# A two-layer graph kernel: four near one-hot buffers, distances a pair ahead of the lanes, sums two superchunks behind, one-hots with the lane innermost, and index loads cut into 96 rows

## The chip, the cores and the metric

The kernel runs on one core of one Trainium2 chip. The metric is device time in microseconds (us). "Before" is the kernel as it stood, "after" the changed one. A core has five engines that run their own instruction streams and meet at semaphores: TensorE (PE, with its weight loads as PEld), VectorE (DVE), ScalarE (ACT), GpSimd (POOL) and SyncE (SP), which issues most of the DMAs.

## The reference, cut to what matters

```python
# x: (6250, 64); src, dst: (200000,), sorted by dst; edge_attr: (200000, 2, 64)
zmax = max(x, axis=-1)
e0, e1 = e[:, 0, :], e[:, 1, :]
q = 0.95 * zmax[src] * e1 + e0
sum_q, sum_ac = segment_sum(q, dst), segment_sum(e1, dst)
z_new = 0.2 * x + 0.8 * sum_q / (sum_ac + 1e-6)
x = layernorm(x + where(deg > 0, z_new, x))
# second layer: 4-head graph attention over the same edges with x @ Wq, x @ Wk, x @ Wv,
# softmax over the edges of one receiver, mean over heads, @ Wout
x = layernorm(x + gat(x))
```

The change touches only the first layer, above all the gather `zmax[src]` and the three segment sums (q, e1, and the degree), and the loads of `src` and `dst` at the start.

## The kernel before, in words

**Start.** SyncE loads `src` and `dst` as [98, 2048] words (196 superchunks of 1024 edges, two to a row): 97 full rows in one DMA, the last row, which holds 1344 words, in a second (L287 to L290). It then issues `x` (L292, L293) and the weights. VectorE turns `src` into two four-bit codes and their squared length (L558 to L568), which go to a DRAM scratch `codes_dram`, and `dst` into positions relative to a window of 24 nodes, plus tables of windows (L572 to L606). TensorE and ScalarE turn both around so that edges lie on partitions (L1194, L992). VectorE then waits for TensorE's turned `dst` (L615), makes the bf16 table of `zmax` in three parts (L627 to L633) and the loop starts.

**First layer.** One loop goes over the 196 superchunks t: 28 written out, then six turns of a body of 28. For one superchunk:

- SyncE loads its 512 KB of edge attributes into one of S1 = 7 slots (L327) and, every fourth, the code rows (L320).
- TensorE, `distances` (L1219): four matmuls, for two superchunks at a time, give the distance of every edge's code to each of 128 codes in PSUM (psD, all four of its banks hold one pair).
- ScalarE, `near_step` (L1014): two activations with Relu make of these the bf16 one-hot `near`, over 128 rows of the table of zmax. Two buffers.
- TensorE, `lanes` (L1225): 24 matmuls with `near` as weights and the table as moving operand give the 49 candidates of each edge in psZ.
- VectorE, `sums_step`: multiplies the candidates with the one-hot of the right lane (`picked`, L679, 392 elements), makes the one-hot of the receiver in its window (`hots`, L655), reduces `picked` to zmax per edge (`zm`, L685), adds sums that TensorE finished earlier into `acc` in two halves (L664), and between these makes the lane one-hot of the next superchunk (`hi_hots`, L659).
- GpSimd, `present_step`: weighs the receiver one-hot with zm (`hz_done`, L441) and counts degrees (L455 to L462).
- TensorE, `sums_of` (L1234): 64 matmuls with the edge attributes as weights and the two one-hots as moving operand.

**Order and waits.** Every engine's order is written out in the program. On TensorE step k is lanes(k), sums(k - 1), and on even k the distances of superchunks k + 2 and k + 3. The sums of k - 1 wait for GpSimd's product (`hz_done`) and for VectorE's adds (`add_done`), lanes(k) for ScalarE's near and for the pick of k - 2. ScalarE's near(k) waits for the pick of k - 2 (`sel_done`).

**After the loop** come the fold of the sums and the layer norm (to about 800 us) and the attention layer, which the change leaves alone.

## Time and profile before

| | |
|---|---|
| Time, median of 3 runs | 2893.26 us (2886.39 to 2896.32) |
| The profiled execution, own time | 2893.56 us |
| Its span, first to last instruction | 2891.3 us |
| Mean granted TensorE clock over the span | 0.709 |
| Busy over the span | PE 74%, PEld 54%, DVE 61%, ACT 45%, POOL 66% |
| Start, to the first lanes | 112.3 us |
| First layer's loop, 196 superchunks | 112 to 748 us |

The page gives shares over the whole span, in which the attention layer weighs most. The change lies in the first 750 us, so the two stages at the top of the list, the start and the loop, have to be read apart. A clock of 1.0 means the whole time at the higher of the two levels of TensorE's clock (2.4 GHz), 0.5 the whole time at the lower (1.2 GHz).

### The profile page before, as it was taken

The numbers are of one execution on the slowest core, as the hardware profiler recorded it, in microseconds if no ns is written. First come the engines' busy times: TensorE is split into PE (matmuls) and PEld (weight loads), VectorE is DVE, ScalarE is ACT, GpSimd is POOL, SyncE is SP. The second block draws the span as 40 slices with busy tenths as digits, with TensorE's granted clock in tenths as the row PEclk, the third lists the DMA queues.
The fourth block names the chain that finished last, engine by engine and source line by source line (L and its number), as shares of the span: only waits on it lengthen the run. The fifth ranks groups of instructions, "written<-read, shape, count | busy, mean of one in ns | idle before, by whom it ended". The sixth has DMA issues, their size and how long they took to land.

```text
span 2891.3 us, 78363 instructions
## 1 busy us (share of the span) xinstructions
PE 2144.7 (74%) x25183; PEld 1557.5 (54%) x25184; DVE 1768.1 (61%) x6022; ACT 1310.4 (45%) x3789; POOL 1896.0 (66%) x2644
## 2 busy tenths in 40 slices
PE   0476776666878787878877878878787877778875
PEld 0365665555746555545545555545565545555554
DVE  2676666676775655555556655655555555656568
ACT  0344333343364444444545544545444444545443
POOL 1355554455677777777777777777777777777750
PEclk9978777787675766676567666776656677776577
DMA  1455555455212122221222212222122221222111
GB/s 43 136 176 178 165 161 164 157 176 165 62 31 43 33 43 44 43 43 36 43 43 43 44 36 43 44 43 43 37 43 43 43 43 36 43 43 43 36 20 24
DMA packets 175709, 197.71 MB, mean 68 GB/s; under 512 B 95155, under 2 KB 97891, under 8 KB 173217
## 3 DMA queue, kind: packets, MB, share of 16 engines
q1 hardware_dynamic: 125030, 138.90, 16.8%
q0 software_dynamic: 50048, 51.35, 9.6%
q8 instruction: 280, 4.59, 0.7%
q14 instruction: 351, 2.88, 0.3%
HBM read 184.87 MB, written 5.25 MB: 66 GB/s over the span
## 4 chain that ended last, share of the span: by engine, by line
POOL 33%; PE 25%; issue 21%; DVE 9%; DMA 6%; SPq 3%; DVEq 1%; ACT 1%; ACTq 0%; POOLq 0%
POOL XS L518 32%; DMA XS<-x_dram,dst_bs 6%; PE psN L1234 3%; PE psS L1397 3%; PE psV L1356 3%; PE psM L1356 3%; PE psX L1225 2%; PE psM L1234 2%; PE psV L1225 2%; PE psT L1351 2%; DVE zm L685 1%; POOL XS L441 1%; DVE O L806 1%; PE psX L1346 1%; PE psN L1346 1%
## 5 line engine op out<-in xcount | busy, mean ns | idle before, releaser
L518 POOL DMA_INDIRECT XS<-x_dram,dst_bs x1564 | 1492.1, 954 | 487.9 <-issue 445.6
L803 DVE SCALAR_TENSOR_TENSOR l_st<-l_st,alpha,rsum 64x1 f32 x782 | 169.5, 217 | 552.7 <-PE psV L1356 279.7
L1397 PE MATMUL psS<-XT,Ubuf 96*128 96x512 f32 x522 | 417.1, 894 | 18.7 <-ACT Ubuf L1084 18.4
L875 DVE TENSOR_REDUCE rmax<-psS 128x1 f32<-128x512 f32 x391 | 270.2, 691 | 39.6 <-issue 16.2
L1356 PEld LDWEIGHTS psV<-XS,PT 128*128 128x128 f32 x1568 | 285.0, 271 | 1.4 <-ACT PT L1133 1.2
L1356 PE MATMUL psV<-XS,PT 128*128 128x64 f32 x1568 | 284.6, 346 | 0.7 <-ACT PT L1133 0.7
L1356 PEld LDWEIGHTS psM<-XS,dst_bs 128*128 128x128 f32 x1560 | 281.5, 270 | 1.6 <-ACT dst_bs L1133 1.6
L1356 PE MATMUL psM<-XS,dst_bs 128*128 128x64 f32 x1560 | 281.6, 345 | 0.7 <-ACT dst_bs L1133 0.7
L1133 ACT COPY PT<-psT 128x512 f32<-128x512 f32 x196 | 114.7, 585 | 349.6 <-PE psT L1351 349.0
L441 POOL TENSOR_TENSOR XS<-XS,zm 128x192 f32<-128x192 f32 x196 | 115.9, 592 | 239.1 <-DVE zm L685 237.7
L1133 ACT COPY dst_bs<-psT 128x512 f32<-128x512 f32 x195 | 114.1, 585 | 343.8 <-PE psT L1351 340.1
L1346 PEld LDWEIGHTS psX<-ident,XS 128*128 128x128 f32 x392 | 58.1, 184 | 390.1 <-issue 388.5
L1346 PEld LDWEIGHTS psN<-ident,XS 128*128 128x128 f32 x390 | 57.6, 183 | 380.8 <-issue 379.6
L1346 PE MATMUL psX<-ident,XS 128*128 128x128 f32 x392 | 108.5, 372 | 163.5 <-DMA XS<-x_dram,dst_bs 160.1
L1346 PE MATMUL psN<-ident,XS 128*128 128x128 f32 x390 | 107.1, 369 | 157.4 <-DMA XS<-x_dram,dst_bs 151.9
L1397 PE MATMUL psS<-dst_bs,Ubuf 96*128 96x512 f32 x260 | 210.0, 903 | 7.9 <-ACT Ubuf L1084 7.9
L1014 ACT ACTIVATE dst_bs<-psA,code_c 128x512 bf16<-128x512 f32 x98 | 67.3, 687 | 319.6 <-PE psT L1219 318.5
L1123 ACT ACTIVATE dst_bs<-psS,cur 128x512 f32<-128x512 f32 x195 | 134.0, 687 | 140.0 <-DVE cur L891 125.2
L1123 ACT ACTIVATE Pm<-psS,cur 128x512 f32<-128x512 f32 x196 | 134.7, 687 | 121.3 <-DVE cur L891 120.5
L797 DVE TENSOR_SCALAR XT<-big,win_ids 32x512 f32<-32x512 f32 x269 | 131.5, 489 | 73.6 <-issue 72.3
L1351 PE MATMUL psT<-ident,dst_bs 128*128 128x128 f32 x780 | 171.7, 362 | 5.1 <-ACT dst_bs L1123 4.8
L1351 PE MATMUL psT<-ident,Pm 128*128 128x128 f32 x784 | 173.1, 363 | 2.2 <-ACT Pm L1123 2.1
(276 smaller groups left out, 4408.6 us busy)
## 6 DMA issues: line engine op xcount, KB each, us to landing
big<-in_edge_attr_2x SPq DMA_DIRECT2D x195, 512.0 KB, 4.0
big<-dst_turned SPq DMA_DIRECT2D x49, 512.0 KB
XS<-x_dram,dst_bs POOLq DMA_INDIRECT x1564, 2.5
O<-codes_dram SPq DMA_DIRECT2D x200, 6.0 KB
x_dram<-x SPq DMA_DIRECT2D x12, 128.0 KB, 1.9
out<-big SPq DMA_DIRECT2D x12, 128.0 KB
codes_dram<-O SPq DMA_DIRECT2D x3, 392.0 KB
dst_turned<-big SPq DMA_DIRECT2D x1, 784.0 KB
```

Of the source, the lines that this page charges most:

```text
L441: return pool.tensor_tensor(buf[:, :, W:2 * W], buf[:, :, 0:W], z[:, :].unsqueeze(2).broadcast_to([P, SJ, W]), ALU.mult)
L518: pool.indirect_dma_start(xs(k, j), None, x1_dram, bass.IndirectOffsetOnAxis(ap=idx2[b % SB][:, k * CPP + j:k * CPP + j + 1], axis=0)).the ...
L797: dve.tensor_scalar(t[D:96, :], dst_b[J // S2 % SB][:, J % S2 * CH:(J % S2 + 1) * CH], ids, None, ALU.not_equal).then_inc(s, 1)
L803: dve.scalar_tensor_tensor(out=ls, in0=ls, scalar=al[half], in1=rs[half], op0=ALU.mult, op1=ALU.add)
L875: dve.tensor_reduce(rmax[:, q:q + 1], psSc[q][:, :], AX_X, ALU.max)
L1123: act.activation(Pms[a][:, :], psSc[a][:, :], ACT.Exp, bias=cur[:, a:a + 1], accum_out=rsum[:, a:a + 1]).then_inc(exp_done, 1)
L1133: act.copy(PTs[a][:, :], psT[:, :]).then_inc(pt_done, 1)
L1234: last = pe.matmul(ps[q * QT:(q + 1) * QT, h * 2 * W:h * 2 * W + n], e_sb[slot][:, h, c, q * QT:(q + 1) * QT], buf[:, j, 0:n], start=(c == ...
L1346: last = pe.transpose(psXc[b][:, j * P:(j + 1) * P], two, ident[:, :])
L1351: last = pe.transpose(ps[:, j * P:(j + 1) * P], probs[:, j * P:(j + 1) * P], ident[:, :])
L1356: last = pe.matmul(ps, pt[:, j * P:(j + 1) * P], xs(k, j), start=(j == 0), stop=(j == CPP - 1))
L1397: pe.matmul(psSc[1 - a][:, :], Ubuf[1 - a][:, :], XT[(J - 1) % 3][:, :], start=True, stop=True).then_inc(s_done, 1)
```

## The change

1. `near` has four buffers in place of two; ScalarE waits for the lanes of k - 4 (`z_done`), no longer for the pick of k - 2. `hz` has four buffers too.
2. TensorE's step k is: on even k the distances of k + 2 and k + 3, then lanes(k), then sums(k - 2). VectorE adds the sums of k - 3 in step k (before: k - 2).
3. `hi_hot` is laid out (edge group, lane) in place of (lane, edge group), so that the pick reads it in one run, and its making reads `hi_col` with the innermost step 0.
4. The [98, 2048] loads and stores are 96 rows, and the last two rows apart, each cut into 16 (or 8) pieces.

```diff
-        near = [dst_bs[:, k * CH:(k + 1) * CH].bitcast(BF16) for k in range(2)]
+        near = [t.bitcast(BF16) for t in (dst_bs[:, 0:CH], dst_bs[:, CH:2 * CH], XS[:, S2 * CPP * D - CH:S2 * CPP * D], dst_bs[:, 3 * CH:4 * CH])]
...
+            TM = TP_ // 16 * 16
+
+            def load_words(t, flat, done):
+                sp.dma_start(t[0:TM, :], flat[0:TM * RE].rearrange("(a b) -> a b", b=RE)).then_inc(done, 16)
+                for r in range(TM, TP_):
+                    n = RE if r < TP_ - 1 else LR
+                    sp.dma_start(t[r:r + 1, 0:n].rearrange("a (k e) -> a k e", k=16),
+                                 flat[r * RE:r * RE + n].rearrange("(a k e) -> a k e", a=1, k=16)).then_inc(done, 16)
+
             sp.wait_ge(s_init, 1)
-            sp.dma_start(src_raw[0:TP_ - 1, :], src[0:(TP_ - 1) * RE].rearrange("(a b) -> a b", b=RE)).then_inc(s_sall, 16)
...
+            load_words(src_raw, src, s_sall)
+            load_words(dst_raw, dst, s_dall)
...
-                    sp.wait_ge(seg_done, seg0 + (t - S1 + 3))
+                    sp.wait_ge(seg_done, seg0 + (t - S1 + 4))
...
-            for s, n in ((sel_done, 2), (hz_done, 1), (half_added, 2), (add_done, 3), (seg_done, 2), (deg_read, 2), (deg_done, 1), (s_pass, 1)):
+            for s, n in ((z_done, 4), (sel_done, 2), (hz_done, 2), (half_added, 3), (add_done, 4), (seg_done, 3), (deg_read, 2), (deg_done, 1), (s_pass, 1)):
...
             def hi_hots(t, q):
-                dve.tensor_tensor(hi_hot[q].rearrange("p (w j) -> p w j", j=SJ), lane_ids.rearrange("p (w j) -> p w j", j=SJ),
-                                  hi_col[:, bass.ds(t, 1), :].broadcast_to([P, LANES, SJ]), ALU.is_equal).then_inc(hi_done, 1)
+                dve.tensor_tensor(hi_hot[q].rearrange("p (j w) -> p j w", j=SJ), lane_ids.rearrange("p (j w) -> p j w", j=SJ),
+                                  hi_col[:, bass.ds(t, 1), :].rearrange("p s j -> p (s j)").unsqueeze(2).broadcast_to([P, SJ, LANES]), ALU.is_equal).then_inc(hi_done, 1)
...
-                dve.tensor_tensor(picked[k % 2].rearrange("p (j w) -> p j w", j=SJ), psZ[k % 2][:, 0:SJ * LANES].rearrange("p (j w) -> p j w", j=SJ),
-                                  hi_hot[k % 2].rearrange("p (w j) -> p j w", j=SJ), ALU.mult).then_inc(sel_done, 1)
+                dve.tensor_tensor(picked[k % 2], psZ[k % 2][:, 0:SJ * LANES], hi_hot[k % 2], ALU.mult).then_inc(sel_done, 1)
...
-                act.wait_ge(sel_done, vv)
+                act.wait_ge(z_done, vv)
...
-                pe.wait_ge(oh_done, vv)
-                pe.wait_ge(sel_done, vv)
-                lanes(k)
-                if not (isinstance(t, int) and t < 1):
-                    sums_step(k - 1, vv)
                 if k % 2 == 0:
                     u = (k + 2) // 2
                     nxt = pe.snap(vv + 1, min_val=1)
@@
                     pe.wait_ge(oh_done, nxt)
                     distances(u // 2 % RQ, u % 2)
+                pe.wait_ge(oh_done, vv)
+                pe.wait_ge(sel_done, vv)
+                lanes(k)
+                if not (isinstance(t, int) and t < 2):
+                    sums_step(k - 2, vv)
```

In the order of instructions, first SyncE at the start of the program, where the index words are loaded (97x2048 is partitions by words). Before:

```order
L287 DMA big<-in_src 97x2048
L288 DMA big<-in_src 1x1344
L289 DMA O<-in_dst 97x2048
L290 DMA O<-in_dst 1x1344
L292 DMA x<-in_x 128x48x64
```

After:

```order
L290 DMA big<-in_src 96x2048
L293 DMA big<-in_src 1x2048
L293 DMA big<-in_src 1x1344
L290 DMA O<-in_dst 96x2048
L293 DMA O<-in_dst 1x2048
L293 DMA O<-in_dst 1x1344
L300 DMA x<-in_x 128x48x64
```

Two more DMAs stand ahead of `x`, and the large ones have 96 partitions. Next TensorE at the start of the loop (psA, psS, psT and psS1, printed as psS, are the distances; psV and psX the lanes; psM the sums). Before:

```order
L1219 MATMUL psA<-O,code_w 128x512
L1219 MATMUL psS<-O,code_w 128x512 x2
L1219 MATMUL psT<-O,code_w 128x512
L1225 MATMUL psV<-table,dst_bs 128x49 x24
L1266 REGISTER_ALU
L1219 MATMUL psA<-O,code_w 128x512
L1219 MATMUL psS<-O,code_w 128x512 x2
L1219 MATMUL psT<-O,code_w 128x512
L1268 ISA
L1225 MATMUL psX<-table,dst_bs 128x49 x24
L1234 MATMUL psM<-XS,big 32x24 x2
```

After:

```order
L1230 MATMUL psT<-O,code_w 128x512
L1236 MATMUL psV<-table,dst_bs 128x49 x24
L1279 ISA
L1236 MATMUL psX<-table,dst_bs 128x49 x24
L1279 ISA
L1272 REGISTER_ALU
L1230 MATMUL psA<-O,code_w 128x512
L1230 MATMUL psS<-O,code_w 128x512 x2
L1230 MATMUL psT<-O,code_w 128x512
L1236 MATMUL psV<-table,XS 128x49 x24
L1245 MATMUL psM<-XS,big 32x24 x2
```

The first sums now stand behind the lanes of superchunk 2, not 1, and the distances ahead of the even lanes; the number of matmuls is the same. Last VectorE in the loop (Pm, PT: picked; XS: the receiver one-hot; PmX: the lane one-hot; big: acc). Before:

```order
L679 TENSOR_TENSOR Pm<-psV,PmX 128x392
L655 TENSOR_TENSOR XS<-win_rel,O 128x8x24
L685 TENSOR_REDUCE zm<-Pm 128x8
L664 ISA
L664 TENSOR_TENSOR big<-big,psM 128x2x24
L659 TENSOR_TENSOR PmX<-dst_bs,O 128x392
L664 ISA
L664 TENSOR_TENSOR big<-big,psM 128x2x24
```

After:

```order
L689 TENSOR_TENSOR PT<-psX,PmX 128x392
L665 TENSOR_TENSOR XS<-win_rel,O 128x8x24
L694 TENSOR_REDUCE zm<-PT 128x8
L674 ISA
L674 TENSOR_TENSOR big<-big,psM 128x2x24
L669 TENSOR_TENSOR PmX<-dst_bs,O 128x392
L674 ISA
L674 TENSOR_TENSOR big<-big,psM 128x2x24
```

The order within a step is the same; the sums in psM, of an even superchunk, are now added beside the pick of an odd one.

## Rows read from the trace of the kernel before

**Rows 1.** Busy time by stretch: PE, PEld, DVE, ACT, POOL (instructions), granted clock, DMA share, GB/s.

```profile
7.00:37.00 30.00, 0.00 (x0) 0.00 (x0) 0.55 (x2) 0.00 (x0) 8.56 (x2) 1.00 0.06 26
112.00:748.00 636.00, 448.55 (x17581) 371.86 (x17585) 432.06 (x1172) 250.56 (x392) 332.01 (x977) 0.79 0.53 169
```

**Rows 2.** Timeline, first two issues of SyncE (start us, us, what).

```profile
5.53 0.36 SPq L287 DMA_DIRECT2D big<-in_src  x1
5.95 8.29 SPq L288 DMA_DIRECT2D big<-in_src  x1
```

**Rows 3.** Timeline from the start to the first lanes.

```profile
4.88 10.64 POOL L428 MEMSET big<- 128x12640 f32 x1
...
37.70 1.23 DVE L558 TENSOR_SCALAR big<-big 98x2048 int32<-98x2048 int32 x1 [30.10 <-DMA big<-in_src]
...
70.38 1.23 DVE L572 CAST big<-O 98x2048 f32<-98x2048 int32 x1 [20.80 <-DMA O<-in_dst]
...
84.48 5.37 POOL L432 MEMSET O<- 128x6320 f32 x1 [68.92 <-DMA codes_dram<-O]
84.52 5.35 DVE L600 TENSOR_SCALAR lohi_i<-lohi_i 98x4 int32<-98x4 int32 x1
...
97.52 0.17 DVE L615 MEMSET big<- 128x128 f32 x1 [5.76 <-PE psM L1194]
...
112.33 1.18 PE L1225 MATMUL psV<-table,dst_bs 128*128 128x49 bf16 x24 [1.46 <-ACT dst_bs L1014]
```

**Rows 4.** Waits of TensorE in the loop (us in total, times, longest).

```profile
PE psN L1234 <- POOL XS L441: 25.0, 36, 1.8
PE psM L1234 <- POOL XS L441: 21.7, 30, 0.9
```

**Rows 5.** Timeline of TensorE, 298 to 308 us.

```profile
298.36 0.38 PE L1219 MATMUL psA<-O,code_w 3*128 3x512 bf16 x1
...
302.49 0.70 PE L1234 MATMUL psM<-XS,big 128*32 128x48 f32 x43 [1.76 <-issue]
303.13 0.82 PE L1225 MATMUL psV<-table,dst_bs 128*128 128x49 bf16 x24
303.87 1.35 PE L1234 MATMUL psN<-XS,big 128*32 128x24 f32 x59
306.19 0.38 PE L1234 MATMUL psN<-XS,big 128*32 128x24 f32 x5 [0.97 <-issue]
```

**Rows 6.** Timeline of TensorE, 464 to 476 us.

```profile
464.76 1.51 PE L1234 MATMUL psN<-XS,big 128*32 128x24 f32 x64
...
466.75 1.18 PE L1225 MATMUL psX<-table,dst_bs 128*128 128x49 bf16 x24
467.85 0.89 PE L1234 MATMUL psM<-XS,big 128*32 128x24 f32 x64
474.07 1.16 PE L1225 MATMUL psV<-table,dst_bs 128*128 128x49 bf16 x24 [5.33 <-issue]
```

**Rows 7.** Timeline of one superchunk's chain, all engines.

```profile
402.15 0.88 DVE L679 TENSOR_TENSOR Pm<-psV,PmX 128x392 f32<-128x392 f32 x1 [0.55 <-PE psV L1225]
...
403.33 0.56 DVE L685 TENSOR_REDUCE zm<-Pm 128x8 f32<-128x392 f32 x1
...
403.92 0.35 DVE L659 TENSOR_TENSOR PmX<-dst_bs,O 128x392 bf16<-128x392 bf16 x1
404.05 0.59 POOL L441 TENSOR_TENSOR XS<-XS,zm 128x192 f32<-128x192 f32 x1 [0.66 <-DVE zm L685]
...
404.19 0.20 DVE L664 TENSOR_TENSOR big<-big,psM 128x48 f32 x1
...
404.70 0.41 PEld L1234 LDWEIGHTS psM<-XS,big 128*32 128x32 f32 x34 [0.61 <-POOL XS L441]
```

**Rows 8.** DMA between 120 and 740 us: instruction queue, edge loads.

```profile
q8 instruction: 147, 2.41, 1.7%
...
big<-in_edge_attr_2x SPq DMA_DIRECT2D x187, 512.0 KB, 4.0
```

More of the change, by code:

```diff
@@ L51, in gnn_resnorm_kernel @@
     SB = 3
+    HB4 = 4
     U2 = 48
@@ L134, in gnn_resnorm_kernel @@
         hi_i = XS[0:TP_, 0:RE].bitcast(I32)
-        hz = [XS[:, k * SJ * 2 * W:(k + 1) * SJ * 2 * W].rearrange("p (j w) -> p j w", j=SJ) for k in range(3)]
-        hzX = hz[2]
+        hz = [XS[:, k * SJ * 2 * W:(k + 1) * SJ * 2 * W].rearrange("p (j w) -> p j w", j=SJ) for k in range(HB4)]
         dst_bs = sb("dst_bs", [P, 4 * CH], I32)
@@ L175, in gnn_resnorm_kernel @@
         relX = sb("relX", [P, SJ])
-        part = dst_bs[:, 3 * CH:3 * CH + 7 * W].bitcast(F32)
+        part2 = Pm[:, SJ * LANES:SJ * LANES + 4 * W]
+        part1 = PT[:, SJ * LANES:SJ * LANES + 2 * W]
         ones = sb("ones", [P, 1])
@@ L443, in present_step @@
             def present_step(t, k):
[L445 to L447 removed]
+                h2 = part2.rearrange("p (h j w) -> p h j w", h=2, j=2)
+                h1 = part1.rearrange("p (h w) -> p h w", h=2)
+                hot4 = hz[k % HB4].rearrange("p (h j) w -> p h j w", h=2)
                 vv = pool.snap(pcc, min_val=1)
@@ L690, in sums_step @@
                     dve.wait_ge(half_added, vv)
-                    add_sums(lb, psG[k % 2], 1).then_inc(add_done, 1)
+                    add_sums(lb, psG[(k + 1) % 2], 1).then_inc(add_done, 1)
                 dve.reg_add(tc, tc, 1)
@@ L1011, in near_step @@
                     act.reg_add(bc, bc, 1)
-                act.wait_ge(sel_done, vv)
+                act.wait_ge(z_done, vv)
                 for h in range(2):
-                    last = act.activation(near[k % 2][:, h * CH:(h + 1) * CH], psD[k % 2][h][:, :], ACT.Relu,
+                    last = act.activation(near[k % 4][:, h * CH:(h + 1) * CH], psD[k % 2][h][:, :], ACT.Relu,
                                           bias=code_c[:, 3:4], scale=-1.0)
@@ L1060, in keep_turned @@
                 act.copy(xt1[u % 2][0:rows_, 0:n], u_turn[u % 2][0:rows_, 0:n]).then_inc(s_xTc, 1)
-            act.wait_ge(s_dsts, 16)
+            act.wait_ge(s_dsts, 32)
             keep_turned(0)
@@ L1224, in lanes @@
                     for c in range(3):
-                        last = pe.matmul(psZ[k % 2][:, j * LANES:(j + 1) * LANES], near[k % 2][:, j * P:(j + 1) * P], table3[:, c, :],
+                        last = pe.matmul(psZ[k % 2][:, j * LANES:(j + 1) * LANES], near[k % 4][:, j * P:(j + 1) * P], table3[:, c, :],
                                          start=(c == 0), stop=(c == 2))
@@ L1284, in _ @@
                             step(i * UN + (HEAD + k), HEAD + k)
-                sums_step(NS - 1, pe.snap(pc, min_val=1))
+                left = pe.snap(pc, min_val=1)
+                sums_step(NS - 2, left)
+                sums_step(NS - 1, pe.snap(left + 1, min_val=1))
             pe.wait_ge(s_all1, 2)
```

62 lines of the change are left out of this document (30 added, 32 removed).

## The prediction, on record before the changed kernel ran

> **What bounds the kernel now.** I read the page for the stages, then busy time by stretch, then the timeline of the start, then TensorE's waits and its timeline in the loop. The change can act in two places: the 112.3 us ahead of the first lanes and the 636 us of the loop; behind 748 us the program is the same.
>
> At the start hardly anything computes. Between 7 and 37 us the DMA share is 0.06, one engine's worth of 16, and 26 GB/s flow [rows 1]: the load of `src` issued at 5.53 us [rows 2] is on one engine, and the first operation on it starts at 37.70 us, after 30.10 us of idle time. The same happens to `dst`: the cast L572 starts at 70.38 us after 20.80 us idle [rows 3]. Later VectorE waits 5.76 us at L615 for TensorE's turned `dst` [rows 3].
>
> In the loop TensorE is busy 448.6 of 636 us at a mean clock of 0.79 [rows 1], that is 58% of the time at the high level (0.5 + 0.5 x 0.58). The other 187 us are, by its waits, 46.7 us at the sums for GpSimd's product [rows 4], and nearly all the rest is "issue", for which the profile has no releaser. This issue time has two forms. One is in the middle of a group of equal matmuls: 1.76 us in front of 43 sums and 0.97 us in front of the last 5 of 64 [rows 5]. Between these two resumptions are 43 + 24 + 59 = 126 matmuls and 3.70 us. The instruction queue moved 147 blocks, 2.41 MB, in 620 us [rows 8], so one block of 16 KB per 4.2 us, about once for each such run of matmuls. I read these stalls as TensorE waiting for its next block of instructions. A superchunk has 24 + 64 + 2 = 90 matmuls, so a block holds 1.4 superchunks. The other form is the back edge of the body, 5.33 us [rows 6]; five of them are 27 us. What is left for blocks is 187.4 - 46.7 - 27, some 113 us, less a few for ScalarE.
>
> **The change part by part.** *Rows of 96.* No row shows 96 partitions. The bounds: as slow as 97 on one engine, no gain; or like the edge loads, 128 partitions and 512 KB landed 4.0 us after issue [rows 8], from which I estimate 6 us for 768 KB, so `src` is there at 12 us. I take the second. By the Trainium skill ("DMA: Bandwidth & Descriptors", the section "Why a DMA increments its semaphore by 16 and not by 1") a DMA runs on the largest number up to 16 that divides its slowest dimension: one for 97, which the share of 0.06 bears out, and 16 for 96; by it the load takes what I estimate from the edge loads, and no gain is excluded. GpSimd clears `acc` from 4.88 us for 10.64 us [rows 3]. L600, a tensor_scalar of 4 elements, took 5.35 us beside such a memset of 5.37 us [rows 3], so L558, a tensor_scalar too, will not end before the memset does, at 15.5 us, and its own 1.23 us: 16.7 us in place of 38.93. That is 22.2 us. The `src` chain ended 20.80 us ahead of 70.38, at 49.6 us; now at 27.4 us. `dst` has landed by then, the second large load behind the first, so L572 starts there: 43.0 us earlier. L600 stays behind a memset of GpSimd as before, since that waits for the same relative positions; no change. TensorE's second turn waited for `src` being turned, which hung on the weights that SyncE could issue only at 73 us. Now they are issued at about 11 us, and the idle 5.76 us at L615 go too. Together **48.7 us**, and the first lanes at 63.6 us. Bounds: 42 if SyncE's issues of loads run into each other as now (8.29 us for L288 [rows 2]), 53 if GpSimd's memset holds nothing up. The stores of 96 rows lie beside other work; nothing. More small DMAs: a handful of issues of 0.4 us [rows 2] on SyncE, which is then idle; nothing.
>
> *The chain of the sums.* At 402.15 us the pick starts, at 403.33 the reduce (0.56), at 404.05 GpSimd's product (0.59), and at 404.70 TensorE goes on, 0.61 us late: 2.55 us from pick to sums [rows 7]. With sums two behind, the product of k - 1 is no longer wanted, but the adds of step k - 1 still are, since `add_done` frees the PSUM bank. They end at 404.39 [rows 7], 2.24 us behind the pick. So the new release is the second add, 0.31 us sooner than the product, before the layout is counted.
>
> *Lane innermost.* The pick takes 0.88 us for 392 elements, the reduce of the same number 0.56 [rows 7]. Read in one run the pick should take between 0.56 and 0.88; I take 0.58. The making of the one-hot takes 0.35 us for the 392 now [rows 7]; it stays at 0.35 if the step of 0 costs nothing, and goes to 0.56, the pace of the reduce, if it does. I take 0.56, net 0.09 less per step. The skill ("Vector Engine (DVE) Microarchitecture Reference", section "5.1 Performance modes") speaks against this half of the change: two results a cycle want 16-bit operands with innermost step 1, and a two-source operation that read one element again and again ran at one a cycle. By it this edit alone adds 0.2 us times 196, 41 us of VectorE's time, and by the rows at most as much. On the path it is 0.31 + 0.30 - 0.21 = 0.40 us that the sums are released sooner, where the mean wait now is 46.7 us in 66 times, 0.71 us [rows 4]. A good half of the 46.7 us goes directly.
>
> *Four near buffers, distances first.* TensorE's waits for ScalarE are too few to have a row here; nothing directly. The distances now lead their lanes by two steps, and ScalarE, with four activations a pair, has the time. If it were late, TensorE would stop in front of the distances with lanes and sums queued behind; its work between two distances is 2 x (0.82 + 0.89) = 3.4 us at the high clock [rows 5, 6], and four activations are under 3 us.
>
> *What the loop then stands on.* TensorE's work per superchunk is 0.82 + 0.89 + 0.38/2 = 1.9 us at the high clock [rows 5, 6] and 1.18 + 1.51 + 0.3 = 3.0 us at the low one [rows 6]; the 0.3 is half of 0.38 scaled like the lanes. Instruction blocks allow one superchunk per 3.70/1.4 = 2.64 us at best. So the floor is 0.58 x 2.64 + 0.42 x 3.0 = 2.79 us, times 196 is 547, and 27 for the back edges: 574 against 636 us, **at most 62 us**. VectorE's step, 0.58 + 0.35 + 0.56 + 0.56 + 2 x 0.20 = 2.45 less the overlaps of about 0.1 each, is 2.1, below it. Of the 62 I take 43: half of the POOL waits, 24, and 19 because a wait inside a block also puts off the request for the next one. Bounds: 5, where every wait removed turns into a longer block stall, and 66.
>
> The tail gets one more group of sums, +1 us. The sum against the profiled execution's own 2893.6 us (0.3 above the median of the runs): 2893.6 - 48.7 - 43 + 1 = **2803 us**.
>
> **The rivals.** *The loop does not move*: blocks set the pace and shorter waits only lengthen stalls. For it: 113 us of stall are more than twice the POOL waits. Against: at the low clock TensorE has work for 1.4 x 3.0 = 4.2 us per block, more than 3.70, so waits there cost in full. It gives 2893.6 - 48.7 = 2845.
> *Blocks are no floor*: the stalls come from something that the decoupling removes, and the loop falls to VectorE's 2.1 at the high and TensorE's 3.0 at the low clock: 0.58 x 2.1 + 0.42 x 3.0 = 2.48, times 196 plus 27 is 513, 123 us less: 2723. Against: one block per run of 126 matmuls fits too well.
> *The start does not move*, as the loads stay narrow or `x` or the weights take their place: 2893.6 - 43 + 1 = 2852. For it: L288 alone blocked SyncE for 8.29 us [rows 2].
> *Slower*: the new rhythm keeps TensorE at the low clock. Each superchunk then costs 3.0 us of work in place of the mean 2.29 (448.6/196), and the idle 0.96 stays: 3.96 x 196 = 776, 140 us more, and 2893.6 + 140 - 48.7 = 2985. It decides from where work grows by the 48.7 us that the start gives: 0.25 us a superchunk, the high clock's share falling from 0.58 to about 0.36. Against: less waiting means a busier engine.
>
> **How the numbers follow.** Chances: the forecast 0.57, the loop unmoved 0.18, blocks no floor 0.09, the start unmoved 0.07, slower 0.04, and 0.05 for what I have not seen. The forecast's own range is 2780 to 2830. The range that leaves out two in ten goes from 2893.6 - 53 - 66 = 2775, a little lower for part of the second rival, to the unmoved start at 2852: 2770 to 2852. Within 0.3%, 8.7 us, a measurement of this kernel can't tell a difference from none; that both stages gain nothing has 0.03. Faster 0.93, same 0.03, slower 0.04.
>
> **What would show it.** Right: L572's successor starts near 27 us and the first lanes near 64; a pick of about 0.58 and a lane one-hot of 0.56 us; TensorE's waits for GpSimd gone, and fewer than 25 us for VectorE's adds in their place; stalls inside groups still there, at 3.7 us or more apart; a loop of about 593 us. Wrong: a DMA share of 0.06 at the start, ScalarE late in front of the distances, a clock well below 0.79 in the loop, or stalls gone.

## The result and the profile after

| | before | after |
|---|---|---|
| Time, median of 4 runs each | 2891.49 us (2886.39 to 2896.32) | 2856.12 us (2848.35 to 2856.7) |
| Ratio, 95% interval | | 0.9872 (0.9847 to 0.9896) |
| The profiled execution, own time | 2893.56 us | 2856.21 us |
| Span | 2891.3 us | 2853.6 us |
| First lanes, first row of TensorE's lanes in the timeline | 112.3 us | 65.2 us |
| Loop, from there to the first row of the fold | 640.0 us | 640.2 us |
| From the fold to the end | 2139.0 us | 2148.1 us |

The change gains 35 us of 2891, not the 90 that I forecast, and the median lies 4 us above my range. The start gives the gain (47.1 us); the loop gives nothing. The interval of the ratio leaves out 1, so the gain itself is clear of noise. The last row of the table is work that the change leaves alone; it came out between 2137.4 and 2153.6 us in the thirteen profiles taken on chips of this speed, and I take its 9 us as spread, which is argued and not shown.

The line of busy times of the page after:

```profile
PE 2168.6 (76%) x25183; PEld 1585.8 (56%) x25184; DVE 1756.7 (62%) x6022; ACT 1302.3 (46%) x3789; POOL 1940.1 (68%) x2644
```

The timeline of the start, all engines, which answers to [rows 2, 3]:

```profile
4.66 10.64 POOL L438 MEMSET big<- 128x12640 f32 x1
...
5.53 0.41 SPq L290 DMA_DIRECT2D big<-in_src  x1
6.00 0.59 SPq L293 DMA_DIRECT2D big<-in_src  x2
...
8.79 10.44 SPq L301 DMA_DIRECT2D x<-in_x  x1
11.20 5.22 DVE L568 TENSOR_SCALAR big<-big 98x2048 int32<-98x2048 int32 x1 [3.50 <-DMA big<-in_src]
...
19.27 1.00 SPq L303 DMA_DIRECT2D XT<-in_L_gnn_Wq  x1
...
27.21 1.23 DVE L582 CAST big<-O 98x2048 f32<-98x2048 int32 x1
...
39.58 5.37 POOL L442 MEMSET O<- 128x6320 f32 x1 [24.24 <-DVEq L594]
39.74 5.23 DVE L597 TENSOR_SCALAR wide<-wide 98x4 f32<-98x4 f32 x1
...
48.58 0.17 DVE L625 MEMSET big<- 128x128 f32 x1
...
65.23 1.18 PE L1236 MATMUL psV<-table,dst_bs 128*128 128x49 bf16 x24
```

`src` has landed at 11.20 us in place of 37.70. The first tensor_scalar lasts 5.22 us and ends at 16.4, 1.1 us behind the end of GpSimd's memset at 15.3, as the step said. The cast of `dst` starts at 27.21 us without a wait, and L625, which was L615 and stood behind 5.76 us of idle time [rows 3], has none.

Busy time by stretch, with the columns of [rows 1]: the start, and 636 us from the first lanes on.

```profile
7.00:37.00 30.00, 5.03 (x32) 4.33 (x32) 25.51 (x17) 6.46 (x8) 8.34 (x2) 1.00 0.63 154
65.00:701.00 636.00, 440.19 (x17632) 367.14 (x17629) 413.45 (x1174) 238.92 (x389) 372.46 (x980) 0.82 0.53 168
```

The DMA share of the start is 0.63 where it was 0.06. In the loop TensorE is busy 8 us less and VectorE 19 us less for the same work, and the stretch is as long. So idle time has taken the place of what went. TensorE's waits in the same stretch (us in total, times, longest):

```profile
PE psM L1245 <- issue: 77.7, 69, 2.8
PE psN L1245 <- issue: 52.0, 50, 3.7
PE psV L1236 <- issue: 23.6, 14, 3.6
PE psA L1230 <- issue: 20.0, 6, 4.0
PE psX L1236 <- issue: 15.4, 15, 2.5
PE psV L1236 <- ACT dst_bs L1025: 4.8, 3, 1.6
```

The rows for GpSimd, 25.0 and 21.7 us before [rows 4], are gone. The five rows of "issue" are 189 us. Under "issue" stand two things, stops in the middle of groups, and waits in front of sums whose releaser the profile doesn't name. Of the latter, all 46 in which the first weight load of the sums comes more than 0.12 us late end within 0.12 us of the end of one of VectorE's adds, as forecast; this is one of them:

```profile
284.18 0.20 DVE L674 TENSOR_TENSOR big<-big,psN 128x48 f32 x1
284.45 0.24 PEld L1245 LDWEIGHTS psN<-XS,big 128*32 128x32 f32 x13 [0.84 <-issue]
```

VectorE in the loop, by shape (busy us, mean ns, idle us before):

```profile
L669 DVE TENSOR_TENSOR PmX<-dst_bs,O 128x392 bf16<-128x392 bf16 x196 | 109.8, 560 | 0.0
...
L689 DVE TENSOR_TENSOR Pm<-psV,PmX 128x392 f32<-128x392 f32 x98 | 55.6, 567 | 122.7 <-PE psV L1236 122.4
```

Pick 0.567 us, lane one-hot 0.560, against the forecast 0.58 and 0.56.

For what follows I sorted every idle piece of TensorE in the loop of the trace, over 0.1 us, by the matmul or weight load on both sides: *in a group*, when they have the same line and destination; *in front of* a group otherwise; *long*, when over 3.2 us. What is left of the loop is work.

| us | loop | work | in groups | before sums | before lanes and distances | long |
|---|---|---|---|---|---|---|
| before | 640.0 | 451.3 | 108.2 | 46.9 | 8.2 | 25.3 |
| after | 640.2 | 443.1 | 141.9 | 18.8 | 14.1 | 22.4 |

The wait before sums shrank by 28 us, work by 8, the long pieces by 3. The stalls in groups grew by 34 and those before lanes and distances by 6, and the sum is zero. Before, the long pieces are the five back edges. After, four of the six are back edges, the other two (3.58 and 3.75 us) stand in the middle of groups, and the fifth back edge, 3.19 us, stands one column to the left.

### The profile page after: what moved, and what is told of

Same layout as the page of the kernel before. It is cut to its first block, busy times and chain, and to the rows that moved or that the text cites. A ratio compares the mean times of both kernels' runs of the same rounds, so it can differ in the third digit from the quotient of the medians.

```text
span 2853.6 us, 78268 instructions
## 1 busy us (share of the span) xinstructions
PE 2168.6 (76%) x25183; PEld 1585.8 (56%) x25184; DVE 1756.7 (62%) x6022; ACT 1302.3 (46%) x3789; POOL 1940.1 (68%) x2644
## 4 chain that ended last, share of the span: by engine, by line
POOL 35%; PE 29%; issue 21%; DVE 8%; DMA 5%; ACT 1%; DVEq 1%; ACTq 0%; SPq 0%; POOLq 0%
POOL XS L528 35%; DMA XS<-x_dram,dst_bs 5%; PE psM L1245 4%; PE psN L1245 4%; PE psS L1410 3%; PE psX L1236 3%; PE psV L1236 3%; PE psM L1369 3%; PE psV L1369 3%; PE psT L1364 1%; PE psA L1230 1%; DVE O L817 1%; PE psN L1359 1%; PE psX L1359 1%; DVE XS L758 1%
## 5 line engine op out<-in xcount | busy, mean ns | idle before, releaser
L1410 PE MATMUL psS<-XT,Ubuf 96*128 96x512 f32 x522 | 425.6, 911 | 20.0 <-ACT Ubuf L1095 19.3
L1369 PEld LDWEIGHTS psV<-XS,PT 128*128 128x128 f32 x1568 | 294.6, 279 | 1.4 <-ACT PT L1144 1.2
L1369 PE MATMUL psV<-XS,PT 128*128 128x64 f32 x1568 | 293.0, 353 | 0.7 <-ACT PT L1144 0.7
L1369 PEld LDWEIGHTS psM<-XS,dst_bs 128*128 128x128 f32 x1560 | 292.6, 279 | 1.6 <-ACT dst_bs L1144 1.6
L1369 PE MATMUL psM<-XS,dst_bs 128*128 128x64 f32 x1560 | 291.7, 354 | 0.7 <-ACT dst_bs L1144 0.7
L1144 ACT COPY PT<-psT 128x512 f32<-128x512 f32 x196 | 114.9, 586 | 357.8 <-PE psT L1364 357.2
L451 POOL TENSOR_TENSOR XS<-XS,zm 128x192 f32<-128x192 f32 x196 | 142.9, 729 | 194.4 <-DVE zm L694 185.4
L1134 ACT ACTIVATE dst_bs<-psS,cur 128x512 f32<-128x512 f32 x195 | 134.1, 687 | 137.7 <-DVE cur L902 120.8
L1245 PE MATMUL psM<-XS,big 128*32 128x24 f32 (+1 forms) x6272 | 120.0, 221 | 78.2 <-issue 77.7
```

Source lines behind the costliest of these rows:

```text
L451: return pool.tensor_tensor(buf[:, :, W:2 * W], buf[:, :, 0:W], z[:, :].unsqueeze(2).broadcast_to([P, SJ, W]), ALU.mult)
L1134: act.activation(Pms[a][:, :], psSc[a][:, :], ACT.Exp, bias=cur[:, a:a + 1], accum_out=rsum[:, a:a + 1]).then_inc(exp_done, 1)
L1144: act.copy(PTs[a][:, :], psT[:, :]).then_inc(pt_done, 1)
L1245: last = pe.matmul(ps[q * QT:(q + 1) * QT, h * 2 * W:h * 2 * W + n], e_sb[slot][:, h, c, q * QT:(q + 1) * QT], buf[:, j, 0:n], start=(c == ...
L1369: last = pe.matmul(ps, pt[:, j * P:(j + 1) * P], xs(k, j), start=(j == 0), stop=(j == CPP - 1))
L1410: pe.matmul(psSc[1 - a][:, :], Ubuf[1 - a][:, :], XT[(J - 1) % 3][:, :], start=True, stop=True).then_inc(s_done, 1)
```

## The experiments

All kernels below also carry the change's start (rows of 96) unless said. "Loop" and "in groups" are measured as above, on the profiled execution. Two profiles of the changed kernel gave loops of 640.2 and 635.9 us, two of the kernel with 64-column sums 512.7 and 508.8, so a difference under 5 us in one profile says little.

**1. The start alone, fewer instructions, no back edge.** Four kernels on one chip, whose runs of before have a median of 2892.28 us.

*b_rows96* is the kernel before with part 4 of the change alone.

> The kernel before with part 4 of the change alone (rows of 96). Both theories: the first lanes near 65 us in place of 112, the loop as before (640 us from the first lanes to the first fold), total about 2893 - 47 = 2846 us. If the loop moves too by over 5 us, the loads of the start reach into it and the accounting by stages is wrong.

Measured: 2846.74 us, ratio 0.9835 (0.981 to 0.9859); first lanes at 63.6 us, loop 631.2, in groups 103.7. The start alone gains 45.5 us where the whole change gained 35, though the intervals of the two ratios overlap. The loop missed what I expected: it is 9 us shorter than 640, and 5 was my limit, beyond which the accounting by stages would be wrong. From the fold to the end this profile has 2144.8 us, 6 more than before. So the total came out as worked out in part by luck, and why this loop is 9 us shorter is open; a difference of that size between loops of single profiles carries little.

*a_m64* is the changed kernel with the sums in half as many matmuls, each with 64 columns of edge attributes as weights in place of 32. The same sums are computed.

```diff
-                    for q in range(4):
-                        n = W if q < 2 else 2 * W
-                        last = pe.matmul(ps[q * QT:(q + 1) * QT, h * 2 * W:h * 2 * W + n], e_sb[slot][:, h, c, q * QT:(q + 1) * QT],
+                    for q in range(2):
+                        n = W if q < 1 else 2 * W
+                        last = pe.matmul(ps[q * D:(q + 1) * D, h * 2 * W:h * 2 * W + n], e_sb[slot][:, h, c, q * D:(q + 1) * D],
```

A superchunk has 24 + 64 + 2 = 90 matmuls, each with its weight load, so 180 instructions of this kind; now it has 58 and 116.

> The changed kernel with the sums in two column tiles of 64 in place of four of 32: the same numbers, 16 matmuls in the program where 32 stood, and per superchunk 116 records of matmuls and weight loads in place of 180; the columns that each part of the array streams stay the same. Theory 'instruction blocks pace the loop': a block now holds 2.1 superchunks, 3.7 us per block allow one per 1.7 us, so the work (1.9 us at the high clock, 3.0 at the low) and VectorE's 2.1 us are left; stalls inside groups fall from 149 us to under 40, the loop by 80 to 130 us, total 2730 to 2780. Rival 'two parts of the change cancel in the loop' (the new order costs what the shorter waits give): stalls in the middle of a group have nothing to do with instructions, the loop moves by under 15 us. Rival 'the edge loads pace it': no change at all.

Measured: 2720.97 us, ratio 0.9389 (0.9361 to 0.9417); loop 512.7, in groups 1.3. The loop falls by 127 us, within the 80 to 130 that I named; the total lies 9 us below my 2730 to 2780. TensorE in it, at a back edge and behind:

```profile
200.82 0.59 PE L1236 MATMUL psX<-table,dst_bs 128*128 128x49 bf16 x17
202.02 1.14 PE L1245 MATMUL psN<-XS,big 128*64 128x24 f32 x32 [0.61 <-POOL XS L451]
206.72 0.60 PE L1230 MATMUL psA<-O,code_w 3*128 3x512 bf16 x1 [3.56 <-issue]
...
207.27 1.18 PE L1236 MATMUL psV<-table,dst_bs 128*128 128x49 bf16 x24
208.38 1.95 PE L1245 MATMUL psM<-XS,big 128*64 128x24 f32 x32
```

A group of sums takes longer than with 64 narrow matmuls, at either level of the clock: 1.14 us against 0.89 and 1.95 against 1.51 [rows 6]. So the gain is not that the same sums became cheaper. The stops in groups fell by 141 us; the time in work fell by 23, at a higher clock, and 50 us came back as longer waits before sums (68.4 against 18.8). The instruction queue now moves 98 blocks between 73 and 560 us, one per 5.0 us, where it was one per 4.2 us. The wider window, 66 to 550 us, by engine:

```profile
66.00:550.00 484.00, 395.01 (x10824) 345.02 (x10821) 409.65 (x1118) 227.09 (x376) 350.66 (x933) 0.95 0.69 213
```

VectorE is busy 85% of it (409.65 of 484), TensorE 82% and at a granted clock of 0.95. Of the 171 waits before sums, 130 end within 0.12 us of the end of one of VectorE's adds and 41 behind GpSimd's product.

*b_m64* is b_rows96 with the same edit of the sums.

> The kernel before with part 4 and the sums in column tiles of 64, near one-hots and order as before. Theory 'instruction blocks': with the stalls gone the waits for GpSimd (47 us before) show in full, so the loop is shorter than before but 30 to 60 us longer than that of the changed kernel with the same sums. Rival 'parts cancel': both have the same loop within 10 us, whether or not it is shorter than 640.

Measured: 2748.11 us, ratio 0.9487 (0.9461 to 0.9514); loop 542.5, in groups 5.3. TensorE's largest waits between 66 and 550 us:

```profile
PE psM L1243 <- POOL XS L450: 42.8, 74, 0.9
PE psN L1243 <- POOL XS L450: 31.6, 69, 0.8
```

Here TensorE waits for GpSimd's product, 85.7 us before sums in all. Parts 1 to 3 of the change don't do away with these waits, they make most of them end at VectorE's adds, sooner: 68.4 us are left in a_m64, and its work is 11 us shorter.

*a_unroll* is the changed kernel with all 196 superchunks written out (`UN = 196` in place of 28), so without a back edge.

> The changed kernel with the first layer's body of 28 written out for all 196 superchunks on every engine, so no back edges. Theory: each of the five back edges costs 9.7 us from pick to pick where 3.0 are usual, so the loop is 5 x 6.7 = 34 us shorter, total about 2822; stalls inside groups stay near 149 us. Rival: what stands at the back edge is work that would wait anyway, and under 10 us go.

Measured: 2821.7 us, ratio 0.9745 (0.9721 to 0.9769); loop 605.4, in groups 137.7. Against loops of 640.2 and 635.9 us the five back edges cost 30 to 35 us, 6 to 7 us each. The stalls in groups are not their work.

**2. Parts of the change in the loop.** Four kernels on another chip; before there 2894.14 us.

*after_again* is the changed kernel once more.

> The changed kernel once more, unaltered, beside its parts on one chip: about 2855 us, and the loop within 5 us of 640. How far its loop differs from 640.2 is how far a loop may differ between two profiles for nothing.

Measured: 2853.0 us, ratio 0.9865 (0.9839 to 0.9892); loop 635.9, in groups 144.8.

*p_layout* is b_rows96 with part 3 of the change (the lane innermost: the three statements at L415, L669 and L689). *p_order* is the changed kernel with these three as before, so parts 1, 2 and 4.

> The kernel before with the rows of 96 and the new layout of the lane one-hot (parts 3 and 4), without the new buffers and order. Theory 'instruction blocks pace the loop': 0.1 us less of VectorE's time per superchunk is not on the path, the total is that of the rows of 96 alone, 2847 us, within 6. Rival 'parts cancel': the layout alone makes the loop 10 to 20 us shorter and the order alone as much longer.

> The changed kernel with the old layout of the lane one-hot (parts 1, 2 and 4). Theory 'instruction blocks': within 6 us of the changed kernel, 2850 to 2862. Rival 'parts cancel': 2865 to 2880, as the layout's gain is missing and the order's loss stays.

Measured: p_layout 2842.65 us, ratio 0.983 (0.9803 to 0.9857), loop 627.0, in groups 114.9. p_order 2853.43 us, ratio 0.9868 (0.984 to 0.9896), loop 641.6, in groups 137.1. Against b_rows96 (631.2 and 103.7) the layout moves the loop by -4 us, within what two profiles differ by, and the order by +10. The order removes all waits for GpSimd and adds 33 us of stalls in groups. The layout alone already shows the exchange: 44.8 us before sums become 29.6, and 103.7 in groups become 114.9. On this one chip p_layout and after_again, which differ by parts 1 and 2, are 10 us apart in their runs (2842.65 and 2853.0) and 9 in their loops. So part 2, with the buffers that it needs, costs some 10 us here, and the change would be better without it; the rival 'parts cancel' was half right. These are differences of 0.4%, near what runs of one kernel differ by.

*a_half* loads half of the edge attributes in the 140 superchunks of the body whose slots are reused; the other half of the slot keeps old values, so the sums of these superchunks are not the reference's.

```diff
-                    sp.dma_start(e_sb[slot][:, :, :, :], edge_v[bass.ds(t, 1)]...
+                    hh = slice(0, 2 if isinstance(t, int) else 1)
+                    sp.dma_start(e_sb[slot][:, hh, :, :], edge_v[bass.ds(t, 1), :, hh]...
```

> The changed kernel with half of the edge attributes not loaded in the 140 superchunks of the five middle turns (the second half of each slot keeps what an earlier load left, so its sums are not the reference's). It asks what a block's 3.7 us are made of. Theory 'blocks, with their transfer slowed by edge loads': the transfer of a block of 16 KB takes 1.1 us now and about 0.6 to 0.9 with half the traffic, so the loop is 15 to 35 us shorter, and stalls inside groups stay above 100 us. Rival 'the edge loads themselves pace the loop': the loop falls by 100 us and more. Rival 'the block's time has nothing to do with traffic': under 10 us.

Measured: 2825.47 us, ratio 0.9771 (0.9745 to 0.9796); loop 611.6, in groups 136.0. The loop is 24 to 29 us shorter, but the stalls in groups are 6 to 9 us shorter only. The instruction queue between 73 and 670 us:

```profile
q8 instruction: 148, 2.42, 1.7%
...
big<-in_edge_attr_2x SPq DMA_DIRECT2D x140, 256.0 KB, 2.9
```

And 607 us of its loop by engine, where the granted clock is 0.86 (0.82 in the changed kernel):

```profile
65.00:672.00 607.00, 420.42 (x17600) 351.58 (x17598) 414.14 (x1172) 238.92 (x389) 373.37 (x980) 0.86 0.40 116
```

TensorE is busy 20 us less for the same matmuls, so most of the 24 to 29 us is the higher clock. The loop moved by what the theory said, but not for its reason: the transfer of a block takes 1.11 us on average as in the changed kernel, and not 0.6 to 0.9. Why half of the load raises the clock is open.

**3. The parts again, where blocks don't stop TensorE.** Four kernels on a third chip, where the attention layer of every kernel, before too, took some 570 us longer (before: 3459.97 us) and the first layer as long as elsewhere; so the loops are what is compared.

*m64_order* is p_order and *m64_layout* p_layout with the sums of a_m64; *a_m64_unroll* is a_m64 with `UN = 196`.

> The changed kernel with column tiles of 64, but the old layout of the lane one-hot. VectorE is busy 84% of that loop, so its 0.1 us per superchunk should now be on the path: loop 512.7 + 15 to 25, total 2736 to 2746. Rival: the layout is worth nothing here either, total 2721.

> The kernel before with rows of 96, column tiles of 64 and the new layout, but the old order and buffers. Where blocks don't pace, order and layout should each be worth something: against 542.5 without either and 512.7 with both, I expect a loop of 520 to 532, total 2728 to 2740. Rival: the whole 30 us are the layout's, total 2721; or all are the order's, total 2748.

> The changed kernel with sums in column tiles of 64 and the body written out 196 times: the version that should beat both. Its loop took 512.7 us with back edges, each 7.4 us where 2.44 are usual, so 5 x 4.9 = 25 us less: loop 488, total about 2696 us. Rival: code loading of the other engines, now without back edges too, brings nothing, and under 10 us go.

| us, all with 64-column sums | order as before | order and buffers of the change |
|---|---|---|
| layout as before | b_m64 542.5 | m64_order 529.3 |
| layout of the change | m64_layout 524.7 | a_m64 512.7, 508.8 |

Ratios: m64_order 0.9571 (0.9531 to 0.961), m64_layout 0.9554 (0.9525 to 0.9583), a_m64_unroll 0.9477 (0.9447 to 0.9508). With no stalls in groups the order is worth 12 to 16 us and the layout 17 to 21, together 30 to 34. So the gain that I forecast for the loop, 43 us, exists for the greater part, but not in the kernel that was changed. The five loops are of three chips, one or two profiles for each kernel, and two profiles of one kernel differ by 4 us; on one chip b_m64 and a_m64 are 27 us apart in their runs. a_m64_unroll has a loop of 493.5 us, where I expected 488, 15 to 19 below a_m64.

*a_align* puts 40 increments of an unused semaphore on TensorE's queue ahead of the loop of the changed kernel. They only shift where the body begins in its block.

```diff
+                for _ in range(40):
+                    pe.sem_inc(s_pad, 1)
                 if NS > HEAD:
```

> The changed kernel with 40 increments of an unused semaphore on TensorE ahead of the repeated body, which only shift where the body begins. In the changed kernel TensorE stops twice at a back edge, 3.19 us at the branch and 2.66 us ten matmuls into the lanes, and the pick to pick interval there is 9.7 us, in the kernel before once, 5.16 us, and 7.2. Theory 'the body begins close to the end of a block': shifted, the second stop goes, the interval falls to 7 to 7.5 us, the loop by 10 to 12 us, total 2843. Rival 'the new order costs it' (distances first): the interval stays at 9.7 and the total at 2855.

The changed kernel's TensorE at its first back edge:

```profile
233.13 1.51 PE L1245 MATMUL psN<-XS,big 128*32 128x24 f32 x64
237.83 0.38 PE L1230 MATMUL psA<-O,code_w 3*128 3x512 bf16 x1 [3.19 <-issue]
...
238.16 0.43 PE L1236 MATMUL psV<-table,dst_bs 128*128 128x49 bf16 x10
241.25 0.76 PE L1236 MATMUL psV<-table,dst_bs 128*128 128x49 bf16 x14 [2.66 <-issue]
```

and a_align's:

```profile
238.34 0.46 PE L1246 MATMUL psN<-XS,big 128*32 128x24 f32 x24 [1.22 <-issue]
242.20 0.60 PE L1231 MATMUL psA<-O,code_w 3*128 3x512 bf16 x1 [3.40 <-issue]
...
242.75 1.18 PE L1237 MATMUL psV<-table,dst_bs 128*128 128x49 bf16 x24
243.86 1.51 PE L1246 MATMUL psM<-XS,big 128*32 128x24 f32 x64
```

In the changed kernel a second stop follows 14 matmuls behind the first, since the body begins near the end of a block. In a_align it is gone. From pick to pick across a back edge VectorE takes 9.7 us in the changed kernel (3.05 elsewhere) and 7.8 in a_align. The loop is 633.5 us, with 6 us in it in which TensorE passes the 40 increments; ratio 0.9839 (0.981 to 0.9869), with the gain within what two profiles differ by. The second stop is shown; that it is worth some 9 us of the loop is worked out (1.9 x 5 back edges) and not resolved by the total. This kernel also shows what the stops in groups hang on; I come to that below.

**4. The best so far, and a test that missed.** A fourth chip, also with the longer attention layer (before: 3498.43 us).

*best_again* is a_m64_unroll again. *a_m64_pad* is a_m64 with 32 matmuls of one column in front of each lanes, into a column of psZ that nobody reads, so that a superchunk has 180 instructions again.

```diff
             def lanes(k):
+                for _ in range(32):
+                    pe.matmul(psZ[k % 2][0:QT, 511:512], near[k % 4][:, 0:QT], table3[:, 0, 0:1], start=True, stop=True)
```

> The kernel with column tiles of 64 (loop 512.7 us, no stall inside groups), and ahead of every superchunk's lanes 32 matmuls of one column into an unused column of the same bank, 64 records more, so 180 per superchunk as in the changed kernel. Theory 'instruction blocks pace the loop': stalls in the middle of groups come back, over 80 us of them, and the loop returns to 600 us or more. Rival 'the wider tiles made the array's work itself cheaper in some way': no stalls inside groups, and the loop grows only by the 32 small matmuls, for which 25 to 30 ns each are 0.8 to 1.0 us, largely beside VectorE: loop 530 to 600.

> The changed kernel with column tiles of 64 and the body written out 196 times, once more, on a chip whose runs of the kernel before are near 2890 us: on the chip of its first run these took 3460, all of it behind the first layer. Its loop was 493.5 us there, against 512.7 with back edges, so about 2702 us here.

Measured: a_m64_pad ratio 1.045 (1.0412 to 1.0489), loop 840.9, in groups 0.1; best_again ratio 0.9507 (0.948 to 0.9534), loop 494.6. TensorE of a_m64_pad in the middle of the loop:

```profile
300.41 1.01 PE L1235 MATMUL psV<-table,dst_bs 128*32 128x1 bf16 x32
301.35 1.18 PE L1238 MATMUL psV<-table,dst_bs 128*128 128x49 bf16 x24
302.46 1.95 PE L1247 MATMUL psM<-XS,big 128*64 128x24 f32 x32
```

Every group has the duration of the lower level, in the whole loop; the pads alone cost 1.01 us. A superchunk then has 4.4 us of work, more than the 2.64 that a block allows, so neither theory lets one expect a stall. The test doesn't tell instructions from matmuls.

**5. The best on a chip like the first, and wider sums.** Before there: 2890.36 us. *best_third* is a_m64_unroll, *a_m64_again* is a_m64, *a_m128* is the changed kernel with 128 columns of edge attributes per matmul, 16 matmuls a superchunk.

```diff
-                    for q in range(4):
-                        n = W if q < 2 else 2 * W
...
+                    last = pe.matmul(ps[:, h * 2 * W:(h + 1) * 2 * W], e_sb[slot][:, h, c, :],
+                                     buf[:, j, :], start=(c == 0), stop=(c == CPP - 1))
```

> Column tiles of 64 and the body written out 196 times, a third time, beside the same kernel with back edges on one chip. First layer's loop 494 us, 18 us less than with back edges; total about 2702 us where the kernel before takes 2892.

> Column tiles of 64 with back edges once more: loop within 5 us of 512.7, total 2721 where the kernel before takes 2892. The difference to the version without back edges is 18 us by the loops of the profiles.

> The changed kernel with the sums in one tile of 128 columns (the product with the unweighted and the weighted one-hot for all 128 rows; the quarter that the fold never reads is filled too). 84 records per superchunk in place of 116, but no two column groups work side by side. Theory 'instruction blocks, then VectorE': no stalls inside groups either; VectorE's 2.4 us per superchunk stay, and TensorE's work is 16 x about 0.1 us for the sums at the high clock, so the loop is between 505 and 560 us, no gain over tiles of 64. Rival 'the fewer instructions the better': under 500.

Measured: best_third 2708.76 us, ratio 0.9366 (0.9346 to 0.9386), loop 492.8; a_m64_again 2724.15, ratio 0.9421 (0.94 to 0.9442), loop 508.8; a_m128 3155.48, ratio 1.092 (1.0901 to 1.0938), loop 946.6. In a_m128:

```profile
303.44 3.63 PE L1243 MATMUL psN<-XS,big 128*128 128x48 f32 x16
307.00 0.60 PE L1230 MATMUL psA<-O,code_w 3*128 3x512 bf16 x1
...
307.55 1.18 PE L1236 MATMUL psV<-table,dst_bs 128*128 128x49 bf16 x24
308.55 3.63 PE L1243 MATMUL psM<-XS,big 128*128 128x48 f32 x16
```

The 16 wide matmuls take 3.63 us where 32 take 1.95 at the same level, and TensorE never stops. Fewer instructions help only as long as the work stays as it is; my expectation for this kernel was wrong.

## Why the prediction was right in its parts and wrong in its sum

**The start: right.** 63.6 us was forecast; b_rows96 has 63.6, the change 65.2, since its order puts the second pair of distances ahead of the first lanes. The large load is spread, VectorE is held up to the end of the memset, L582 starts at 27.2 us where I said "near 27". The risk of SyncE's issues was real: L301, the 106-row end of `x`, blocked SyncE for 10.44 us, so the weights went out at 19.3 us and not at 11; it cost nothing, since VectorE had no wait left at L625.

**The single steps of the loop: right.** The pick and the one-hot have the forecast durations; the waits for GpSimd are gone; what stands before sums is 18.8 us for VectorE's adds, under the 25 that I named; ScalarE is not late (4.8 us). The stalls in groups are still there. The rate too: 147 blocks in 620 us before, and 147 between 73 and 693 us after.

**The step that failed: "Of the 62 I take 43: half of the POOL waits, 24, and 19 because a wait inside a block also puts off the request for the next one."** The 43 us measured 0 (640.0 and 640.2). The first 24 came as forecast, as 28 us less before sums, and were lost again; the 19 had the wrong sign, since the stalls in groups grew by 34. That is the lower bound that I had named, "where every wait removed turns into a longer block stall".

The floor under them was too low as well. It took 3.70 us per block from one pair of stops [rows 5]; in the trace after, 77 pairs of stops at neighbouring places are 3.44 to 6.05 us apart, the median 4.17, and before 55 pairs have a median of 4.11. With 4.1 the same working gives 0.58 x 2.93 + 0.42 x 3.0 = 2.96 us, times 196 plus 27 some 607, so at most 33 us to gain and not 62 (an estimate). The upper bound of 66 stood above the 62 besides.

The trace shows where the time went, in another way than by totals. These are the stalls in groups over 0.5 us in the first half of each of the six turns of the body: position, counted in matmuls from a fixed place in the body, and length in us (from matmul to matmul, so a stop right in front of the first matmul of a group isn't in the lists). Before:

```
0 [(133, 1.3), (257, 1.3), (383, 0.8), (632, 1.2), (756, 1.1), (881, 1.5), (1256, 0.9)]
1 [(9, 0.9), (257, 1.8), (383, 1.0), (632, 1.2), (756, 1.1), (881, 1.3), (1256, 1.5)]
2 [(9, 0.9), (257, 1.5), (383, 0.5), (632, 1.0), (881, 1.0), (1006, 0.5), (1131, 0.6), (1256, 1.6)]
3 [(9, 0.8), (257, 1.5), (383, 1.0), (632, 1.6), (756, 1.4), (881, 0.7), (1131, 2.1)]
4 [(9, 0.9), (257, 0.9), (383, 1.8), (881, 1.2), (1006, 1.2), (1131, 2.3)]
5 [(9, 0.7), (257, 1.5), (383, 0.7), (632, 1.0), (756, 1.1), (881, 1.0), (1131, 2.1)]
```

After:

```
0 [(15, 1.5), (140, 2.1), (515, 1.5), (766, 1.6), (890, 0.9), (1015, 1.9), (1265, 0.9)]
1 [(140, 1.6), (390, 0.7), (766, 1.3), (890, 1.4), (1265, 1.7)]
2 [(140, 2.2), (515, 1.3), (640, 1.3), (766, 1.6), (1015, 1.8), (1265, 1.8)]
3 [(140, 1.2), (390, 1.6), (640, 1.5), (766, 1.6), (890, 1.2), (1015, 0.9), (1265, 0.8)]
4 [(140, 1.4), (390, 0.7), (640, 2.1), (766, 1.6), (1015, 1.4), (1265, 1.2)]
5 [(390, 1.6), (515, 0.8), (766, 0.8), (890, 1.2), (1015, 0.8), (1265, 1.2)]
```

They fall on the same instructions in every turn, 124 to 126 matmuls apart or a multiple of it, in the middle of groups that wait for no semaphore. After, one more stands at 264 in each turn, right in front of the first sums: 1.2, 2.4, 1.5, 1.3, 2.2 and 2.8 us. And a_align, whose body differs in nothing, but which has 40 more instructions ahead of it (three of its turns):

```
1 [(121, 1.7), (371, 1.5), (746, 2.0), (1122, 2.5)]
2 [(121, 1.2), (246, 1.0), (371, 2.3), (746, 1.1), (996, 2.3), (1122, 1.0)]
3 [(121, 1.4), (371, 1.5), (496, 1.0), (746, 1.3), (871, 1.2), (996, 0.9), (1122, 1.6)]
```

140, 390, 515 and 766 have become 121, 371, 496 and 746: the stops came 19 or 20 matmuls earlier. 20 matmuls with their weight loads are 40 instructions. So the stops sit at fixed counts of instructions, every 250 or so, and neither data nor the width of a matmul decides their place.

That they are waits for a block of instructions can be read from the transfers of the instruction queue, which the trace holds one by one. In the changed kernel's loop all 88 stops in groups over 0.5 us end between 1.22 and 1.58 us behind the end of a transfer of 16 KB, before all 87 between 1.08 and 1.62; the transfers themselves are 4.2 us apart on average and take 1.1 us. And the next transfer starts 1.4 us (the median) behind the end of such a stop; between the two, TensorE had waited for nothing in 100 of 118 cases. So the next block was mostly on its way before TensorE came to a wait inside this one, which speaks against the reason that I gave for the 19 us.

At many boundaries of a turn there is no stop: the next block was there in time, as behind a longer wait. Before, such waits were the ones for GpSimd; the change took them away and the boundaries took the time back: 28 us less before sums, 34 more in groups. Of these some 11 are the second stop of the back edge (position 2410 of this count: 1.0 at the entry into the body, then 2.7, 1.7, 1.7, 2.3 and 2.0 us) and the rest longer or more frequent stops at boundaries.

The Trainium skill ("Runtime: NRT & Kernel Launch", the section "Instruction fetch mechanics") has blocks of 16 KiB with 256 instructions each, which the trace bears out: 2.41 MB in 147 blocks [rows 8], and 126 matmuls with 126 weight loads between two stops. It calls the cost of crossing one "mostly hidden"; here the stops at them cost 104 to 145 us of loops of 627 to 642, so the measurement decides.

**The rival that happened** is "the loop does not move", 2845 us, to which I gave 0.18; the 11 us above it are 1.6 at the first lanes and 9 behind the fold. What I had held against it, that at the low clock "TensorE has work for 1.4 x 3.0 = 4.2 us per block, more than 3.70, so waits there cost in full", did not save it. TensorE did work at a higher clock (0.82 against 0.79), and the 8 us that its work became shorter are among those that came back as stalls.

**"Blocks are no floor" was wrong as I put it, and its number is met by chance.** Without stalls in groups the loop is 513 us, the very time that I had worked out for that rival. But it needs the instructions cut by a third, not the change, and the terms are others: I had 2.1 us at the high clock for 58% of the time and 3.0 for the rest. In a_m64 the clock is 0.95, with which the same working gives 0.9 x 2.1 + 0.1 x 3.4 = 2.2 us, a loop of some 465; the median from pick to pick is 2.48 us.

What is shown: the start's gain, its place and size; that the loop's waits moved into stops at fixed instructions, which end 1.2 to 1.6 us behind the transfer of a block; that with 116 in place of 180 instructions a superchunk these stops vanish though each group of sums takes longer; that order and layout are worth 30 us then. What is argued only: that a_m64's stops went because it has fewer instructions and not through another effect of its wider weights; its block every 5.0 us agrees with it, and a_m64_pad, which should have brought the stops back with the instructions, had another bound. Open: what sets the times of 1.4 us around a transfer, what half of the edge loads freed, why b_rows96's loop is 9 us shorter, and how much of the 10 us that the new order costs in p_order is the second stop (some 9 by a_align, in which the total did not resolve it).

## What to carry to other kernels

Where idle time of TensorE stands in the middle of a group of equal matmuls, look whether it returns at the same instructions in each turn of a loop; if so the instruction stream sets the pace there, and removing waits on data gives little or, as here, nothing, since each wait was also time for the next block. Cut instructions first (here 64-column weights: 127 us) and then do the decoupling, whose 30 us appear only behind it. The best version of these, 64-column sums and the loop written out, takes 2708.8 us, 0.9366 of before. A back edge costs 3 to 7 us (the written-out loops), and has two stops if the body begins shortly before the end of a block.

## What the runs showed of the hardware that I had not expected

- TensorE can be busy nearly without a break and stay at the lower level: in a_m64_pad and a_m128 lanes of 24 matmuls took 1.18 us all through the loop, as in the low stretches before [rows 6], with PE busy 476 and 481 of the 484 us between 66 and 550. The profile's column of granted clock has 1.00 there, since it holds no record of the clock before 905 and 1080 us; the durations are what tells the level:

```profile
66.00:550.00 484.00, 480.98 (x4252) 453.89 (x4249) 213.41 (x606) 123.22 (x205) 191.64 (x510) 1.00 0.38 117
```

- Forty semaphore increments on TensorE's queue took 6 us (147.5 to 153.6 us of a_align), so they are no free filler. That is 0.15 us each at most, since a block boundary falls among them: a transfer ends at 147.7 us.
- With the new layout GpSimd's product took longer in some kernels and not in others: on average 0.73 us after and 0.70 in p_layout against 0.58 in p_order and 0.59 before, but 0.57 in a_m64 and 0.53 in m64_layout, which have the layout too. So it hangs on what runs beside it; on what, isn't shown. It is off the path in the changed kernel, but in best_third, with 0.67, it is what TensorE waits for most, 40.9 and 19.7 us between 66 and 550:

```profile
PE psN L1245 <- POOL XS L451: 40.9, 65, 0.8
PE psM L1245 <- POOL XS L451: 19.7, 60, 0.6
```

- A DMA of 106 rows of `x` held SyncE for 10.44 us at its issue, where one of 96 rows of `src` with 768 KB took 0.41. The shape alone doesn't set it: before, behind the narrow loads, the same issue took 28.42 us.
